# A third score bank in an attention loop, and turned outputs and maxima that leave TensorE

## The reference

```python
h = tok_ref(x)                               # linear token mixing with a 1024 x 1024 gate, PReLU
h = h + attn_ref(layernorm(h))               # 8 heads of 8 channels, 1024 tokens, relative bias
h = h + ffn_ref(layernorm(h))                # router, top 2 of 8 experts, 64 -> 128 -> 64, exact gelu

attn = einsum('bnhd,bmhd->bhnm', q * scale, k)
attn = softmax(attn + bias, axis=-1)         # bias from rpb_table by the distance of the tokens
out = einsum('bhnm,bmhd->bnhd', attn, v) @ proj_w + proj_b
```

## Time and profile before

| | |
|---|---|
| median of 3 runs | 698.26 us (697.87 to 698.61) |
| the profiled execution | 700.25 us, span 698.5 us |
| TensorE busy | 653.6 us, 94% |
| VectorE busy | 485.8 us, 70% |
| ScalarE busy | 379.2 us, 54% |
| GpSimd busy | 74.4 us, 11% |
| granted TensorE clock, mean | 0.951 |

### The profile page before, as it was taken

How to read it: one execution, slowest core, us unless ns; L and a number is a source line. 1 busy time by engine, 2 the same in 40 slices (tenths; PEclk the granted TensorE clock), 3 DMA queues, 4 the chain that set the end, 5 groups by cost and what they waited for, 6 DMA issues and landing times. The chain is left out here.

```text
span 698.5 us, 13275 instructions
## 1 busy us (share of the span) xinstructions
PE 653.6 (94%) x4374; PEld 216.6 (31%) x4374; DVE 485.8 (70%) x631; ACT 379.2 (54%) x712; POOL 74.4 (11%) x186
## 2 busy tenths in 40 slices
PE   9999899876699999999999999999999976999997
PEld 4323233222122333333333333333323322333332
DVE  4354453636978888888888888888886658574543
ACT  2102212021377777777777778787877624465443
POOL 8501010101200000000000000000000202000000
PEclk9999998975599999999999999999999977999999
DMA  8200554041411212121212121212120020200000
GB/s 301 58 3 0 151 143 130 22 115 49 139 37 37 74 37 73 36 72 36 72 36 72 36 72 36 72 36 72 36 73 3 1 61 0 56 20 8 17 8 15
DMA packets 42961, 40.46 MB, mean 58 GB/s; under 512 B 21777, under 2 KB 32178, under 8 KB 42930
## 3 DMA queue, kind: packets, MB, share of 16 engines
q1 hardware_dynamic: 42930, 40.05, 20.1%
HBM read 26.16 MB, written 11.58 MB: 54 GB/s over the span
## 5 line engine op out<-in xcount | busy, mean ns | idle before, releaser
L805 DVE TENSOR_REDUCE nmax<-ps 128x1 f32<-128x1024 f32 x256 | 311.7, 1222 | 54.7 <-PE ps L1139 38.4
L639 ACT ACTIVATE probs<-ps 128x512 f32<-128x512 f32 x512 | 278.0, 595 | 100.6 <-PE ps L1233 73.4
L1248 PE MATMUL ps<-probs,v_ring 128*32 128x256 f32 x2048 | 166.0, 397 | 0.0
L1233 PE MATMUL ps<-q_ring,k_ring 51*128 51x512 bf16 x512 | 156.5, 392 | 2.8
L1139 PE MATMUL ps<-k_ring,q_ring 48*128 48x512 bf16 x512 | 133.7, 399 | 9.7 <-DVE nmax L805 9.6
L1233 PEld LDWEIGHTS ps<-q_ring,k_ring 51*128 51x128 bf16 x512 | 43.5, 93 | 127.6 <-ACT probs L639 91.2
L1040 DVE TENSOR_TENSOR probs<-probs,ps 128x512 f32<-128x512 f32 x64 | 41.2, 683 | 46.6 <-ACT probs L708 46.5
L1122 PE MATMUL ps<-g_t,x_all 96*128 96x512 f32 x128 | 65.0, 626 | 5.2 <-DVE gated L820 5.2
L1248 PEld LDWEIGHTS ps<-probs,v_ring 128*32 128x32 f32 x2048 | 40.7, 108 | 92.8 <-issue 78.9
L708 ACT ACTIVATE probs<-ps,wide_w 128x512 f32<-128x512 f32 x64 | 40.4, 683 | 47.4 <-PE ps L1400 47.3
L820 DVE TENSOR_TENSOR gated<-ps,gamma_sb 128x512 f32<-128x512 f32 x64 | 42.6, 686 | 32.3 <-PE ps L1122 32.2
(11 more groups left out here) (174 smaller groups left out, 438.9 us busy)
## 6 DMA issues: line engine op xcount, KB each, us to landing
k_ring<-qk_parts SPq DMA_DIRECT2D x64, 96.0 KB, 2.4
q_ring<-qk_parts SPq DMA_DIRECT2D x64, 96.0 KB, 2.4
gamma_sb<-gamma_t SPq DMA_DIRECT2D x4, 1024.0 KB, 10.0
v_padded<-v_pad SPq DMA_DIRECT2D x4, 1024.0 KB, 4.7
v_ring<-v_padded SPq DMA_DIRECT2D x32, 128.0 KB, 2.8
qk_parts<-qk_h SPq DMA_DIRECT2D x8, 384.0 KB, 4.3
x_ring<-bias_parts SPq DMA_DIRECT2D x32, 96.0 KB, 3.1
qk_parts<-qk_m SPq DMA_DIRECT2D x8, 256.0 KB, 3.9
```

Of the source, the lines that this page charges most:

```text
L639: A.activation(probs[:, s % 4, HALF * j:HALF * (j + 1)], ps[:, S2A + j, :], ACT.Exp).then_inc(exp_done[j], 1)
L805: V.tensor_reduce(nmax[:, par, s:s + 1], ps[:, bank:bank + 2, :].rearrange("p a n -> p (a n)"), AX, ALU.max, negate=True).then_inc(s1_redu ...
L1233: last = mm(ps[:, S2A + j, :], k_ring[rows, u, P * s:P * (s + 1)], q_ring[rows, u, HALF * j:HALF * (j + 1)], start=True, stop=not corner)
L1248: last = mm(ps[VC * j:VC * (j + 1), PVB, 0:2 * P], v_ring[:, u, m, :], probs[:, m % 4, 2 * P * j:2 * P * (j + 1)], start=(m == 0), stop=(m ...
```

## The change

- Scores by key get three PSUM banks: half 0 alternates between banks 4 and 5, half 1 has bank 6; the values' bank moves to 7. TensorE issues half 0 of step s + 1 together with half 1 of step s, ahead of the scores by query and the values. Its wait for the maxima rows of the next head moves from the start of that head's round to step 7 of the one before.
- The split maxima are turned by a 32 x 32 block transpose on VectorE, after its second maximum of a round, instead of a transpose on TensorE and a copy on ScalarE. Since four blocks of 32 columns lie in different rows then, SyncE sends them with eight DMAs of 12 rows x 32 values instead of two of 12 rows x 128.
- The output of a head, with its sums, goes from `o_t` (now two buffers) to DRAM scratch in one DMA per head, issued between the sends and the loads. The transposes on TensorE and the division on VectorE go. For each batch, sums are loaded, inverted on VectorE, stored, and loaded again spread over the rows; the outputs are loaded already turned; GpSimd multiplies them (`scale_attention`). Batches 0 to 2 do so in the last four rounds, batch 3 behind the last round, ahead of the copies of input parts in SyncE's queue.
- The projection needs no turning back: 8 small matmuls a batch write it in the layout of the residual. Its bias is spread by one matmul in the first stage and added to h by GpSimd. The projection of batch 3 moves behind the first `up` of the experts.

```diff
+        S1A, S2A, PVB = 0, 4, 7
+        def key_bank(s, j):
+            return S2A + (2 if j else s % 2)
...
-            def send_max_rows(n, u):
-                sp.wait_ge(max_copied, n + 1)
-                half = PARTS * NT // 2
+            def send_max_rows(turned, par, u):
+                sp.wait_ge(max_turned[par], turned + 2)
                 for j in range(2):
-                    sp.dma_start(q_ring[UPPER * j + ROWS:UPPER * j + MAXROWS, u, HALF * j:HALF * (j + 1)],
-                                 max_t[half * j:half * (j + 1), :]).then_inc(max_rows[u], 16)
+                    for a in range(4):
+                        rows = q_ring[UPPER * j + ROWS:UPPER * j + MAXROWS, u, HALF * j:HALF * (j + 1)].rearrange(
+                            "i (m a r) -> i m a r", a=4, r=SQ)
+                        first = SQ * a + PARTS * NT // 2 * j
+                        sp.dma_start(rows[:, :, a, :], max_t[first:first + PARTS * NT // 2, par, :]
+                                     ).then_inc(max_rows[u], 16)
+            def store_output(copied, par, g, u):
+                sp.wait_ge(o_copied[u], copied)
+                sp.dma_start(o_scratch[ds(g, 1), :, :].rearrange("o x (j q) -> o j x q", j=4), o_t[:, par, :]
+                             ).then_inc(o_stored[par], 16)
+            def load_sums(b):
+                sp.dma_start(sums[:, b, :], o_scratch[NH * b:NH * (b + 1), DH, :].rearrange("h (r q) -> h r q", q=D)
+                             ).then_inc(sums_loaded[b // (B - 1)], 16)
+                for j in range(2):
+                    sp.dma_start(ao_all[D * j:D * (j + 1), b, :],
+                                 o_scratch[NH * b:NH * (b + 1), 0:DH, HALF * j:HALF * (j + 1)]
+                                 ).then_inc(ao_loaded[b // (B - 1)], 16)
+            def store_inverse(b):
+                sp.wait_ge(sums_inverted, b + 1)
...
+            def load_inverse(b):
+                sp.wait_ge(inverse_stored[b // (B - 1)], 16 * (1 if b == B - 1 else B - 1))
...
             def attend_sp(it, first, last):
                 for u in range(RING):
                     if not (last and u == RING - 1):
-                        send_max_rows(it * RING + (u + 1), (u + 1) % RING)
+                        send_max_rows(it * 2 + (u + 1) // 2, (u + 1) % 2, (u + 1) % RING)
+                    if not (first and u == 0):
+                        store_output(it + (2 if u else 1), (u - 1) % 2, it * RING + (u - 1), (u - 1) % RING)
                     if not (first and u == 0) and not (last and u > 0):
-                        sp.wait_ge(o_copied[(u - 1) % RING], it + (2 if u else 1))
                         load_head(it * RING + (u - 1 + RING), (u - 1) % RING)
+                    if last and u == 0:
+                        for i in range(2):
+                            sp.wait_ge(o_stored[i], 16 * (G - NH) // 2 + 1)
+                        for b in range(B - 1):
+                            load_sums(b)
+                    if last and u == 1:
+                        for b in range(B - 1):
+                            store_inverse(b)
+                        for b in range(B - 1):
+                            load_inverse(b)
...
             attend_sp(G // RING - 1, False, True)
+            store_output(G // RING + 1, (RING - 1) % 2, G - 1, RING - 1)
+            for i in range(2):
+                sp.wait_ge(o_stored[i], 16 * G // 2 + 1)
+            load_sums(B - 1)
+            store_inverse(B - 1)
+            load_inverse(B - 1)
...
+            def turn_maxima(n, par, sent):
+                dve.wait_ge(max_split, n + 1)
+                if sent is not None:
+                    dve.wait_ge(max_rows[sent[0]], sent[1])
+                V.transpose(max_t[:, par, :], max_p[:, par, :]).then_inc(max_turned[par], 1)
...
-                        if s == 5 and not (first and u == 0):
-                            normalize(g - 1)
+                        if s == 1 and not (last and u == RING - 1):
+                            sent = (u - 1) % RING
+                            turn_maxima(g + 1, (u + 1) % 2, None if first and u == 0 else
+                                        (sent, it * N_MAX_ROWS + (N_MAX_ROWS if u else 0)))
...
             def attend_pe(it, first, last):
...
-                    pe.wait_ge(max_rows[u], it * 32 + 32)
+                    v = (u + 1) % RING
                     pe.wait_ge(values_loaded[u], it * 16 + 16)
                     if ahead:
                         pe.wait_ge(operands[(u + 2) % RING],
                                    (it + (u + 2) // RING) * (16 * N_OPERANDS) + 16 * N_OPERANDS)
+                    if start:
+                        pe.wait_ge(max_rows[u], N_MAX_ROWS)
+                        scores_by_key(0, u, 0)
                     for s in range(NT):
+                        if s == NT - 1 and not end:
+                            pe.wait_ge(max_rows[v], (it + (u + 1) // RING) * N_MAX_ROWS + N_MAX_ROWS)
                         for j in range(2):
-                            scores_by_key(g, s, u, j)
+                            pe.wait_ge(exp_done[j], g * NT + (s + 1))
+                        scores_by_key(s, u, 1)
+                        if s + 1 < NT:
+                            scores_by_key(s + 1, u, 0)
+                        elif not end:
+                            scores_by_key(0, v, 0)
...
-            WITHIN = {(2, 0): [(turn_attention, 0)], (2, 1): [(project_attention, 0)], (2, 3): [(turn_projection, 0)],
-                      (2, 4): [(turn_attention, 1)], (2, 6): [(project_attention, 1)],
-                      (3, 0): [(turn_projection, 1)], (3, 2): [(turn_norm, 0)], (3, 3): [(turn_attention, 2)],
-                      (3, 5): [(turn_norm, 1)], (3, 6): [(project_attention, 2)], (3, 7): [(turn_projection, 2)]}
+            WITHIN = {(2, 2): [(project_attention, 0)], (2, 4): [(project_attention, 1)],
+                      (2, 7): [(project_attention, 2)], (3, 0): [(turn_norm, 0)], (3, 4): [(turn_norm, 1)]}
...
                         if start and e2 == 0:
                             up(n, 0)
+                            project_attention(B - 1)
+                            pe.wait_ge(res_seq, B - 1)
+                            up(n, 1)
                             pe.wait_ge(res_seq, B)
-                            up(n, 1)
                             turn_weights(0)
```

More of the change, by code:

```diff
@@ L528, in _, with scale_attention @@
                 split_maxima(g2)
-            for b in range(B):
+            def scale_attention(b):
+                pool.wait_ge(ao_loaded[b // (B - 1)], 4 * 16 * (1 if b == B - 1 else B - 1))
+                gp.tensor_tensor(ao_all[:, b, :], ao_all[:, b, :], inv_all[:, b, :], ALU.mult).then_inc(ao_scaled, 1)
+            for b in range(B - 1):
+                scale_attention(b)
+            for b in range(B - 1):
                 power(B + b).then_inc(rstd_ready, 1)
+            scale_attention(B - 1)
+            power(2 * B - 1).then_inc(rstd_ready, 1)
             b = B - 2
@@ L575, in _ @@
             leave_v(0)
-            def max_rows_copy(turned, par, sent, sent_slot):
-                act.wait_ge(max_turned[par], turned + 1)
-                if sent is not None:
-                    act.wait_ge(max_rows[sent_slot], sent)
-                A.activation(max_t[:, :], max_ps, ACT.Copy).then_inc(max_copied, 1)
             for b in range(B + 1):
@@ L766, in small_tables @@
                 V.tensor_tensor(b2_p[rows, 2, :], b2_rest[:, :], b2_p[rows, 1, :], ALU.subtract).then_inc(b2_ready, 1)
-                dve.wait_ge(wide_loaded, 16)
-                for j in range(2):
-                    last = V.tensor_copy(proj2[D * j:D * (j + 1), D * j:D * (j + 1)], proj_s[D * j:D * (j + 1), :])
-                last.then_inc(weights_padded, 1)
             def over_d(m):
@@ L826, in _ @@
                         first += 1
+                    if u == 14 and b == B:
+                        turn_maxima(0, 0, None)
                     if b == 0:
@@ L1012, in _ @@
             route_parts(0)
+            add_residual(B - 1)
             center(B - 1)
@@ L1236, in scores_by_key @@
                     for i in range(PARTS):
-                        last = mm(ps[:, S2A, 0:P], x_ring[:, u, i, :], flip_b[:, :], start=False,
+                        last = mm(ps[:, key_bank(s, j), 0:P], x_ring[:, u, i, :], flip_b[:, :], start=False,
                                   stop=(i == PARTS - 1))
@@ L1250, in values, with project_attention @@
                 last.then_inc(pv_done[m % 4], 1)
-            def turn_output(before, copied, maxima):
-                pe.wait_ge(o_copied[before], copied)
-                pe.wait_ge(max_copied, maxima)
-                for c in range(2):
-                    last = nc.tensor.transpose(ps[:, MISC, P * c:P * (c + 1)], o_t[:, P * c:P * (c + 1)], ident[:, :])
-                last.then_inc(o_turned, 1)
-            def turn_attention(b):
+            def project_attention(b):
```

(9 more changed lines are left out.)

183 lines of the change are left out of this document (89 added, 94 removed).

## The result

| | before | after |
|---|---|---|
| median of four runs (lowest to highest), us | 698.07 (692.31 to 698.61) | 886.8 (882.2 to 889.05) |
| profiled execution and its span, us | 700.25, 698.5 | 882.2, 879.6 |
| mean granted clock of the span | 0.95 | 0.825 |

A forecast was written before the change was run, and what follows sets the result against it. Exponentials and matmuls taking turns bound the kernel, with a cycle through SyncE's queue almost as long. Terms + 140 + 1 - 5 + 15 = + 151 on 700.25 gave 851, 849 us by the median; range 740 to 885.

The forecast's parts named there:

- the list at its end: Signs expected in the profile after, such as 256 sends, copies about 16 us apart, TensorE idle, clock below 1.
- the new cycle: Each round: start, maxima, turning, eight sends, store, loads, landing, next start; 16.6 us against 11.59, + 140 over 28 rounds.
- the output store: New store in SyncE's queue between sends and loads: 0.45 us with its gap, upper bound 0.75.
- the landing of x_ring's load: End of each round: the load lands 3.1 us after its issue and TensorE's next round starts.
- Third bank: Scores by key: alone a gain of 1.4 us a head, VectorE then the bound at 10.2 us.
- Start to first send: Each round: sends start 3.8 us after the round's start, with 0.9 more for TensorE's clock falling to 1.2 GHz.
- Eight sends: SyncE's issues of maxima rows in each round: 0.755 us each with the gap, 6.04 us in all.
- cheap-send: Rival for SyncE's sends: 0.45 us each, cycle 13.3, 756 us by the median; at 0.38, 740; chance 0.17.
- dear-send rivals: Rival for SyncE's sends: 1.03 us each, cycle 18.8, 911 us by the median; chance 0.11.
- the rival of a clock that holds: TensorE keeps its clock despite the gap in each round: cycle 15.7, 822 us by the median; chance 0.23.
- Start and last rounds: Ends of attention: first maxima sends cost + 1 us; last three rounds, 42 us against 47, give - 5.
- Handover: From attention to experts: input-part copies wait behind the last DRAM chain, + 13 us, and + 2 for the clock: + 15.

The follow-up runs named there:

- e3_two_sends: The changed kernel with maxima turned as before (TensorE transpose, ScalarE copy) and two sends in place of eight; 707.41 us, 1.014 times before.
- e9_before_store: The kernel before with each output copy also stored to DRAM scratch, between sends and loads, in rounds 1 to 28; 730.89 us, 1.049 times before.

## Why the prediction came out as it did

The mechanism in the changed kernel is as forecast in every sign of the list at its end: 256 sends, eight in a row and 6.00 us long; TensorE released by the x_ring load at the start of rounds; a clock below full; exponentials in unbroken groups; input parts behind the last copy. The size was too small: + 189 by the medians against + 151, and 886.8 lies just above the range's end of 885. What failed are two terms of the new cycle, the output store and the landing of x_ring's load; the first row of the table below is nearly right because two errors in it cancel. The terms, as means of 14 rounds of after between 230 and 520 us (two of them, in which the issue of one load took 1.70 and 0.96 us, are left out of the third row):

| step, us | forecast | measured |
|---|---|---|
| start of round to first send, clock included | 4.7 | 4.86 |
| eight sends | 6.04 | 6.00 |
| store, and on to x_ring's issue | 2.73 | 3.13 |
| x_ring's issue to TensorE's start | 3.1 | 3.59 |
| round | 16.6 | 17.58 |

- **Third bank.** Off the bounding cycle in this change, as said; worth 0.8 us a round once SyncE is out of the way, where I had written 1.4. Its round is then 10.50, near the 10.2 that I had worked out for VectorE, but not for that reason: VectorE is busy for 88% of it and TensorE for 94%. That eight sends leave no room for it held; with two there is room.
- **Start to first send.** Forecast 3.8 and 0.9 for the clock, 4.7; measured 4.86. At full clock the way is 3.42 (the sixteen idle matmuls), since the second maximum ends 3.28 us after the start and not 3.52 as before; the clock adds 1.44. That the sum is right to 0.16 is luck. For the kernel before I also had the way wrong: its sends do not wait for two maxima but for the steps of TensorE, whose transpose runs at 340.13, and for ScalarE's copy behind two more exponentials.
- **Turning on VectorE.** 0.20 us, forecast 0.25, right.
- **Eight sends.** 0.745 to 0.75 with the gap, right, for rows of 64 bytes as for rows of 256; the runs with twelve and with two confirm it from both sides. The cheap-send and dear-send rivals are both out.
- **The output store: the first mis-sized term.** I took 0.45 us, "as the store of padded values"; it is 0.64 and gaps of 0.2 on both sides, 0.40 more. The forecast had the right price in hand as its upper bound, and its argument against it was the cheap bias store. The Trainium skill (DMA: Bandwidth & Descriptors, "Why a DMA increments its semaphore by 16 and not by 1") says that the issuing sequencer writes the increments that a transfer on fewer than 16 engines leaves over. If these writes took time in the queue as the forecast's other sum had it, the total would be 8 us larger. Such a price would fit sends and store (0.70 and 0.64, against 0.36 for a 48-row load), but not for the bias store at 0.33 with its gap, nor for the input parts of 64 rows at 0.60. What sets an issue's price is open; no run tests it.
- **Landing: the second mis-sized term.** The 3.1 us were the median landing, and the forecast let TensorE start in that instant. The median of after is 3.3, and TensorE starts 0.30 us behind the landing on the mean. That is 0.49 us a round. About half of it stood in the rows: from x_ring's issue at 345.74 to the start at 349.08 are 3.34 us. The 0.24 us of spare were misread in the same way (the store put into the kernel before). With the store it makes 0.89, times 28 is 25 of the 26.5 us missed on the rounds.
- **Clock.** Fell in each round, so the rival of a clock that holds is out; its term of 0.9 is 1.2 by the ten idle matmuls and 1.4 by the sixteen.
- **Start and last rounds.** + 1 and - 5, measured - 3.5 and - 1.8: 1.3 us off in sum. The first is 4.5 us off, the second 3.2 the other way; why is open.
- **Handover.** Forecast + 15, measured + 19.9. Three trips of 2.0 us were 3.3, 2.3 and 2.3, and the reciprocal is 0.55: SyncE is free 10.1 us behind the last copy, not 7.2. That is 2.9 of the 4.9 us.
- **Execution and median.** The profiled execution of after is the fastest of its four, 4.6 us under their median, while that of before was 2 us over. The forecast carried before's difference over: 6.6 us of the miss of 37.8.

## What to carry to other kernels

Before you take an operation off a busy engine by turning it into DMAs, count the issues that come with it and find where in their queue they stand: what waits behind them pays for each one in full (0.75 us here), however few bytes it moves. Look for the cycle that closes through a queue (issue, landing, compute, issue) and its spare, and count it to the start of the waiting engine and not to the landing; here it read as 0.24 us, nothing in the waits showed it, and 0.88 us put into it went into the round in full. A sound idea and its costly companion can come in one change: undo the companion alone before the whole is judged, since here the same third bank lies in a kernel that is 27% slower than before and in one that is 4.4% faster.

## What the runs showed of the hardware

- An issue on SyncE's queue of 12 rows of 256 bytes (before, median 0.72) and one of 12 rows of 64 bytes (after, 0.70) take the same time, with 0.05 for the gap. Loads from DRAM of 96 KB take 0.40 into 128 rows (x_ring) and 0.36 to 0.37 into 48 rows (queries and keys). What was not expected is the 0.64 of a 128-partition store to DRAM whose outermost size is 4.
- With a store of 128 KB issued just ahead of it a load of 96 KB has a median landing of 3.2 or 3.3 us (seven kernels), without it of 3.0 or 3.1 (six).
- From the landing to the start of the matmul that waits for it 0.23 to 0.38 us pass (16 rounds of after).
- Waits of some 4 us a round brought the granted clock of the stretch to 0.78; with ten idle matmuls in each wait it was 0.92. With waits of about 1.1 us a round it was 0.99 in one kernel (e3_two_sends) and 0.97 in another (e9_before_store), where 4 of 22 rounds had steps at half clock.
